# First relational layer: messages made for unsorted edges and carried in the scattered rows

## The reference

```python
def _rel_layer(x, src, dst, etypes, V, a, w_loop, bias, activation=None):
    W = jnp.einsum('rb,bio->rio', a, V)
    seg = dst.astype(jnp.int32) * R + etypes.astype(jnp.int32)
    agg = jax.ops.segment_sum(x[src], seg, num_segments=N * R)
    agg = agg.reshape(N, R, -1)
    h = jnp.einsum('nri,rio->no', agg, W) + x @ w_loop + bias
...
h = _rel_layer(h, src, dst, etypes, V1, a1, loop1, b1, activation=jax.nn.relu)
h = _rel_layer(h, src, dst, etypes, V2, a2, loop2, b2, activation=None)
```

## Time and profile before

| | us |
|---|---|
| median of the timed runs | 3510.24 |
| lowest and highest of them (3 runs) | 3508.18, 3512.7 |
| profiled execution: span from the first to the last instruction | 4186.2 |

### The profile page before, as it was taken

How to read it: one execution, slowest core, us unless ns; L and a number is a source line. 1 busy time by engine, 2 the same in 40 slices (tenths; PEclk the granted TensorE clock), 3 DMA queues, 4 the chain that set the end, 5 groups by cost and what they waited for, 6 DMA issues and landing times. The chain is left out here.

```text
span 4186.2 us, 55154 instructions
## 1 busy us (share of the span) xinstructions
PE 2723.7 (65%) x18509; PEld 1820.0 (43%) x18619; DVE 2656.6 (63%) x8007; ACT 533.4 (13%) x1242; POOL 2327.0 (56%) x2253
## 2 busy tenths in 40 slices
PE   0221001898895888957886899999994555555551
PEld 0100001676663676735554566666652222222221
DVE  9001002888854888868887688888854666665667
ACT  0000000000010000000100222222211222222220
POOL 3777774666606666446664566666725444444430
PEclk9555555777765777778887899999985667676665
DMA  5111002111111111111111000000000000000010
GB/s 88 39 37 26 7 7 62 21 21 21 19 62 38 21 22 22 13 22 23 24 24 16 10 10 10 11 10 11 11 4 21 16 17 17 17 17 16 18 14 4
DMA packets 125021, 91.49 MB, mean 22 GB/s; under 512 B 59542, under 2 KB 110678, under 8 KB 124118
## 3 DMA queue, kind: packets, MB, share of 16 engines
q0 software_dynamic: 70912, 41.10, 7.4%
q1 hardware_dynamic: 53846, 46.89, 4.7%
HBM read 60.42 MB, written 27.41 MB: 21 GB/s over the span
## 5 line engine op out<-in xcount | busy, mean ns | idle before, releaser
L732 POOL DMA_INDIRECT rel_rows<-message_table,message_indices x640 | 647.7, 1012 | 449.7 <-issue 173.8
L1287 POOL DMA_INDIRECT flow_x<-node_table,src_indices x440 | 524.9, 1193 | 293.4 <-PE p_x_turned L1406 153.7
L1655 POOL DMA_INDIRECT att_kv_rows<-kv_table,att_index x440 | 417.5, 949 | 474.4 <-DVE att_index L1666 342.7
L795 DVE TENSOR_SCALAR rel_source_onehot<-rel_sources,node_numbers 128x384 bf16<-128x384 f16 x2000 | 547.4, 321 | 208.3 <-remote 174.1
L393 POOL DMA_INDIRECT sorted_edges<-stage,sorted_row x416 | 429.6, 1033 | 191.7 <-issue 126.3
L1429 PE MATMUL flow_acc_bwd<-flow_onehot_j,flow_by_q 128*128 128x309 bf16 (+1 forms) x2530 | 516.9, 335 | 7.1 <-issue 0.2
L870 PE MATMUL p_rel_picked<-rel_source_onehot,rel_h_parts 128*96 128x384 bf16 x2000 | 458.4, 400 | 33.7 <-issue 24.6
L1691 DVE TENSOR_REDUCE att_tile_max<-p_att_scores 128x4 f32<-128x512 f32 x440 | 292.2, 688 | 236.6 <-PE p_att_scores L1805 166.9
L1038 POOL DMA_INDIRECT sum_rows<-node_table,src_indices x280 | 277.5, 991 | 220.5 <-issue 75.0
L870 PEld LDWEIGHTS p_rel_picked<-rel_source_onehot,rel_h_parts 128*96 128x96 bf16 x2000 | 309.2, 155 | 176.6 <-issue 33.3
L1073 DVE TENSOR_SCALAR sum_source_onehot<-sum_sources,node_numbers 128x512 bf16<-128x512 f16 x1000 | 309.1, 377 | 24.8 <-remote 24.8
(11 more groups left out here) (287 smaller groups left out, 4502.7 us busy)
## 6 DMA issues: line engine op xcount, KB each, us to landing
message_table<-message_rows SPq DMA_DIRECT2D x50, 320.0 KB, 2.1
rel_rows<-message_table,message_indices POOLq DMA_INDIRECT x640
rel_sources<-source_rows SPq DMA_DIRECT2D x80, 96.0 KB
flow_x<-node_table,src_indices POOLq DMA_INDIRECT x440
att_kv_rows<-kv_table,att_index POOLq DMA_INDIRECT x440
sorted_edges<-stage,sorted_row POOLq DMA_INDIRECT x416
sum_sources<-source_rows SPq DMA_DIRECT2D x40, 128.0 KB
sum_rows<-node_table,src_indices POOLq DMA_INDIRECT x280
```

The lines of the kernel that those rows point to most:

```text
L732: pool.indirect_dma_start(out=rows[b][:, t, :], out_offset=None, in_=d["messages"], in_offset=bass.IndirectOffsetOnAxis(ap=s["idx_msg"][:, ...
L795: last = dve.tensor_scalar(which[g % 2][:, c, :], srcs[b][:], s["node"][:, c:c + 1], None, ALU.is_equal)
L1287: pool.indirect_dma_start(out=X[b][:, t, 0:F], out_offset=None, in_=d["nodes"], in_offset=bass.IndirectOffsetOnAxis(ap=s["idx_src"][:, g * ...
L1655: pool.indirect_dma_start(out=KV[b][:, t, :], out_offset=None, in_=d["kv"], in_offset=bass.IndirectOffsetOnAxis(ap=ibuf[b][:, t:t + 1], ax ...
```

## The change

The message of an edge doesn't depend on the order of the edges, so the change makes layer 1's messages ahead of the sort's scatter, for the columns of unsorted edges. A group is now 6 of the 416 columns: the messages of 4 are picked by multiplication (one-hots and picks of 512 edges instead of 384), those of 2 are gathered from the table, and the 6 rows of 52 words (20 as before, then the 32 of the message) are scattered. There are 69 groups and a tail of 2 gathered columns, and 6 ring slots of 6 columns each between making and scattering. The table of layer 1 must now be complete before the first gather, so it is made beside the sort: the matrices of both layers on POOL, the copies and the transfers on ACT. `add_sorted` replaces the pass of layer 1: SP loads the sorted rows with messages (20 contiguous loads), DVE makes the one-hots of the destinations, PE adds. Edge rows, indices and block limits for the later layers stand at its end. The rows that no edge fills are written ahead by one SP transfer that repeats a small tile of zeros. `add_up_pass` stays as it was for layer 2, without the branches for layer 1.

```diff
...
-SB = 4
+ROW = REC + F
+CG, CP, SLOTS, RINGS = 6, 4, 6, 4
+CN = EC // CG
+CTAIL = EC - CN * CG
+CW = CP * P
+PADS = 5
+assert CP + CTAIL <= CG and T % PADS == 0
...
+                                 a["L0_gnn_V1"].rearrange("b i o -> i b o")).then_inc(basis_in, 16)
+                sp.dma_start(ab[:], a["L0_gnn_a1"]).then_inc(basis_in, 16)
+                sp.wait_ge(recs, 2)
+                sp.dma_start(d["sorted"][0:T * P, :].rearrange("(p g t) w -> p g (t w)", p=P, t=PADS),
+                             pad[:].rearrange("p t w -> p (t w)").unsqueeze(1)
+                             .to_broadcast([P, T // PADS, PADS * ROW])).then_inc(pads, 16)
...
+                make_weights(pool)
+                second[2](pool)
+
+                for b in range(2):
+                    pool.wait_ge(out[b], 16 * len(range(b, NB, 2)))
+                pool.wait_ge(index_ready, 1)
...
+                def gather(g):
+                    b = g % SLOTS
+                    slot_free(pool, g)
+                    js, c0 = columns(g)
+                    for j in js:
+                        if j >= CP:
+                            c = c0 + j - js[0]
+                            pool.indirect_dma_start(
+                                out=ring[b][:, j, REC:ROW], out_offset=None, in_=d["messages"],
+                                in_offset=bass.IndirectOffsetOnAxis(ap=idx[:, c:c + 1], axis=0))\
+                                .then_inc(gathered[b], 16)
+
+                def scatter(g):
+                    b = g % SLOTS
+                    js, c0 = columns(g)
+                    pool.wait_ge(filled, g + 1)
+                    if g < CN:
+                        pool.wait_ge(msg_ready, g + 1)
+                    pool.wait_ge(gathered[b], 16 * (CG - CP) * (g // SLOTS + 1))
+                    for j in js:
+                        c = c0 + j - js[0]
                         pool.indirect_dma_start(
                             out=d["sorted"], out_offset=bass.IndirectOffsetOnAxis(ap=row[:, c:c + 1], axis=0),
-                            in_=stage[:, c, :], in_offset=None).then_inc(sent[c % SB], 16)
...
+                            in_=ring[b][:, j, :], in_offset=None).then_inc(sent[b], 16)
+
+                gather(0)
+                pool.wait_ge(row_ready, 1)
+                pool.wait_ge(pads, 16)
+                for g in range(CN + 1):
+                    if g < CN:
+                        gather(g + 1)
+                    scatter(g)
+                for b in range(SLOTS):
+                    pool.wait_ge(sent[b], 16 * sum(len(columns(g)[0]) for g in range(b, CN + 1, SLOTS)))
...
+                for b in range(NB):
+                    if b >= 2:
+                        act.wait_ge(out[b % 2], 16 * (b // 2))
+                    for j in range(2):
+                        act.wait_ge(made, 2 * b + j + 1)
+                        act.copy(y[b % 2][:, j * half:(j + 1) * half], py[(2 * b + j) % 3][:, 0:half]).then_inc(got, 1)
+                    act.wait_ge(got, 2 * b + 2)
+                    act.dma_start(d["messages"].rearrange("(n r) f -> n (r f)", r=R)[b * P:(b + 1) * P, :],
+                                  y[b % 2][:]).then_inc(out[b % 2], 16)
...
+                for g in range(CN):
+                    act.wait_ge(pick_done, g + 1)
+                    if g >= 2:
+                        act.wait_ge(z_done, g - 1)
+                    act.copy(gT[g % 2][:], pp[g % 2][0:3 * F, 0:CW]).then_inc(pick_taken, 1)
+                    act.wait_ge(coef_done, g + 1)
+                    if g >= 2:
+                        act.wait_ge(z_taken, g - 1)
+                    act.copy(coef[g % 2][:].rearrange("p t b -> p (t b)"), pc[:, 0:CP * NBASIS]).then_inc(coef_taken, 1)
+                    fill(g)
+                fill(CN)
...
+                dve.wait_ge(ln_std, 1)
+                v.done(dve.reciprocal(stat[:, 3, :], stat[:, 2, :]))
+                dve.scalar_tensor_tensor(out=h3, in0=c3, scalar=0.0, in1=bc(3), op0=ALU.max, op1=ALU.mult)\
+                    .then_inc(h_ready, 1)
+                for b in range(NB):
+                    last = dve.scalar_tensor_tensor(out=rank[:, b, :], in0=rank[:, b, :],
+                                                    scalar=off[:, b:b + 1], in1=mask[:, b, :],
+                                                    op0=ALU.add, op1=ALU.mult)
+                v.done(last)
...
+                dve.tensor_tensor(row[:, FULL:EC], row[:, FULL:EC], extra[:], ALU.add).then_inc(row_ready, 1)
...
+                def sources(g):
+                    b = g % RINGS
+                    dve.wait_ge(row_in[b], 32 * (g // RINGS) + 32)
+                    if g >= 2:
+                        dve.wait_ge(pick_done, g - 1)
+                    for c in range(NB):
+                        last = dve.tensor_scalar(which[g % 2][:, c, :], srcs[b][:], s["node"][:, c:c + 1], None,
+                                                 ALU.is_equal)
+                    last.then_inc(which_ready, 1)
...
+                def types(g):
+                    if g >= 2:
+                        dve.wait_ge(coef_done, g - 1)
+                    dve.tensor_scalar(kinds[g % 2][:], typs[g % RINGS][:], s["lane"][0:R, 0:1], None, ALU.is_equal)\
+                        .then_inc(kinds_ready, 1)
...
+                def weigh(g):
+                    dve.wait_ge(z_done, g + 1)
+                    dve.wait_ge(coef_taken, g + 1)
+                    if g >= 1:
+                        dve.wait_ge(msg_ready, g)
+                    dve.tensor_tensor(terms[:], pz[:, 0:CP * NBASIS * F]
+                                      .rearrange("p (t f b) -> p t f b", b=NBASIS, f=F),
+                                      coef[g % 2][:].unsqueeze(2).to_broadcast([P, CP, F, NBASIS]), ALU.mult)\
+                        .then_inc(z_taken, 1)
+
+                def messages(g):
+                    dve.wait_ge(z_taken, g + 1)
+                    slot_free(dve, g)
+                    dve.tensor_reduce(ring[g % SLOTS][:, 0:CP, REC:ROW], terms[:], AX_X, ALU.add).then_inc(msg_ready, 1)
+
+                for g in range(CN):
+                    sources(g)
+                    if g >= 2:
+                        weigh(g - 2)
+                    types(g)
+                    if g >= 2:
+                        messages(g - 2)
+                for g in range(CN - 2, CN):
+                    weigh(g)
+                    messages(g)
+
...
+                pe.wait_ge(taken, TURNS)
+                pe.wait_ge(w_ready, 1)
+                w2 = W[:].rearrange("p r f -> p (r f)")
+                for n in range(2 * NB):
+                    b, j = divmod(n, 2)
+                    if n >= 3:
+                        pe.wait_ge(got, n - 2)
+                    pe.matmul(py[n % 3][:, 0:half], s["hT"][0:F, b * P:(b + 1) * P], w2[:, j * half:(j + 1) * half],
+                              start=True, stop=True).then_inc(made, 1)
...
+                def pick(g):
+                    pe.wait_ge(which_ready, g + 1)
+                    if g >= 2:
+                        pe.wait_ge(pick_taken, g - 1)
+                    for c in range(NB):
+                        last = pe.matmul(pp[g % 2][0:3 * F, 0:CW], hs[:, c].rearrange("p k f -> p (k f)"),
+                                         which[g % 2][:, c, :], start=(c == 0), stop=(c == NB - 1))
+                    last.then_inc(pick_done, 1)
+
...
+                for g in range(CN):
+                    pick(g)
+                    if g >= 1:
+                        basis_products(g - 1)
+                    coefficients(g)
+                basis_products(CN - 1)
...
+def add_sorted(nc, a, s, d, sb, ps, sem, init, finish):
...
+                    for c in range(LOADS):
+                        b = c % LBUFS
+                        if c >= LBUFS:
+                            sp.wait_ge(used, (c - LBUFS + 1) * per)
+                            sp.wait_ge(rec_taken, c - LBUFS + 1)
+                            sp.wait_ge(dst_taken, c - LBUFS + 1)
+                        sp.dma_start(rows[b][:].rearrange("p t w -> p (t w)"),
+                                     lanes_rows[:, c * LT:(c + 1) * LT, :].rearrange("p t w -> p (t w)"))\
+                            .then_inc(rows_in[b], 16)
...
+                    for c in range(LOADS):
+                        b = c % LBUFS
+                        dve.wait_ge(rows_in[b], 16 * (c // LBUFS) + 16)
+                        dve.tensor_copy(s["dstl"][:, c * LT:(c + 1) * LT], rows[b][:, :, DSTL]).then_inc(dst_taken, 1)
+                        dve.wait_ge(dst_taken, c + 1)
+                        for g in range(c * per, (c + 1) * per):
+                            if g >= HBUFS:
+                                dve.wait_ge(used, g - HBUFS + 1)
+                            dve.tensor_tensor(hot[g % HBUFS][:], lanes[:].unsqueeze(1).to_broadcast([P, RG, P]),
+                                              s["dstl"][:, g * RG:(g + 1) * RG].unsqueeze(2)
```

(64 more changed lines are left out.)

576 lines of the change are left out of this document (333 added, 243 removed).

## The result

The changed kernel takes 3535.98 us (median of 4 runs, 3532.39 to 3541.3) against 3509.21 before: ratio 1.0079, 95% interval 1.0065 to 1.0093. It is 27 us slower, where 55 less had been forecast. The prediction was wrong in the sign of the change.

What follows compares the result with a forecast made beforehand. POOL alone bounded the scatters, mostly DVE and PE pass 1. New terms 120 + 728 + 10 + 40 + 110 = 1008 against 1060; forecast 55 less, 3455 us (1.6%), range 3400 to 3580.

Steps and rivals of the forecast that it cites:

- The part before: Old kernel up to the end of layer 1's pass: 1205 us profiled, taken as 1060 in timed runs.
- The rival of cheaper indirect DMAs: Old scatters: the 0.30 between indirect DMAs is added by profiling; old part 935 against 1008, total 3583; chance 0.06.
- The first gather: Start of the new kernel until layer 1's table is whole: 52 for normalised nodes plus 67 for the table, taken as 120.
- the bound of 150: Upper bound for the first gather, if POOL's 30 matrix instructions hold DVE up for 30 us.
- The groups and the last scatters: New loop: 70 periods of 10.4 us, set by DVE, 728; then one more period, 10, for the last scatters.
- the mean of the earlier trace: One-hots in the new loop at a mean 378 ns each: upper bound of 12.2 a group, 854 in all.
- third rival: New loop: POOL is slowed by DVE's one-hots, 13.5 a group, 946 in place of 728, total 3676; chance 0.05.
- the row of 3.04: Earlier profile row: 10 one-hots of 128x512 took 3.04 with gathers running; gave 7.6 for a group's 25.
- Read-back, limits and the rest: Between and around loop and adds: drain, first load, edge rows, indices and block limits, 40 us, bounds 30 to 60.
- The adds: New stage of 440 adds, two matmuls each, at 0.234 an add: 103, taken as 110 us.
- The fourth rival: Adds take as long as the old pass's last ones: 198 in place of 110, total 3546; chance 0.09.
- point of decision, 162: Length of the adds, 0.37 each, from which the rival of slow adds decides.

Runs made afterwards that it cites:

- the first profile: Profile of the unchanged kernel before, in a slower execution: span 4186.2 us, against a median of 3510.24 in the timed runs.
- the second profile: The kernel before, with no edit, profiled once more in an execution as fast as the timed ones: time 3507.72 us, span 3505.9.

## Why the prediction was wrong, by its own steps

**The part before.** Taken as 1060; measured 1060. Taking out of the first profile what no engine's work explained was right: the second one has 530 for the scatters and 413 for pass 1, where the prediction's deductions leave 526 and 417, and POOL has no wait above 0.3 in the middle of that pass. The rival of cheaper indirect DMAs is out: scatters stand at 0.96 and 0.30 in the second profile too (416 in 530), and that execution lasted as long as the timed ones.

**The first gather: 120, measured 139.** The mechanism that was named for the bound of 150 came: POOL's matrices held up DVE's sort, by 26.5 in the masks (37.00 against 10.46), and the scan held up POOL. What failed is the reason given for leaving this out, that the fill ends before the long steps. The fills run until 8.16, beside the first masks (from 4.47), and cost them some 3 by the comparison above (10.46 against 7.23); the matrices ran from 8.24 to 76.2, beside the rest of the masks and past the scan. The nodes came at 78 in place of 52, and the first gather followed after 61 instead of 67. Moving the matrices gave 24 back in all.

The Trainium skill, page "SBUF — State Buffer", section "Who interferes with whom", has VectorE and GpSimd lock each other out of a shared port pair for a whole instruction, if VectorE's is in a two-port mode, or has two inputs in SBUF while GpSimd's reads SBUF. The trace agrees where both compute: the POOL instruction of 22.93 ends 1.3 after the scan that started 1.2 ahead of it, and 25 masks took 37.00 beside the matrices and 10.46 without them (in which mode the masks ran no row shows). For indirect DMAs the section speaks of GpSimd starved; here it was DVE that paid, 7.65 against 6.63 in a group, with POOL's step unchanged at 1.27.

**The groups and the last scatters: 728 and 10, measured 728 together.** The start-to-start time of the one-hots beside gathers was the right row (0.304 in the sum, 0.306 measured), the mean of the earlier trace rows the wrong one. POOL's starving (third rival) didn't come. That the engines were level is right for DVE and POOL: 10.23 and eight steps of 1.27. The sum took DVE as the longest; in the changed kernel neither waits for the other in the middle of the loop, and POOL ends last. What indirect DMAs cost DVE was already in the row of 3.04, which was taken beside one.

**Read-back, limits and the rest: 40, measured 36.** There are 21.7 from the last scatter's end to the first add and 14 behind the last.

**The adds: 110, measured 188.** This is the step that failed and that turned the sign. Two rows for the same instructions differed by a factor of two, and the sum took the faster one because 440 adds in a row leave PE no pause. That reason is what the runs refute: a PE without a pause did not have the higher clock. In the pass of before, adds stood among picks at a mean clock of 0.83 (1.00 around the row that was used); alone, they run at 0.50 though PE never waits. The fourth rival had the place, the price (198) and the row (the last adds of the pass, behind the last picks), and its point of decision, 162, was passed. Its chance of 0.09 was too low: the row nearest to the new stage, adds with no other work beside them, was the slow one. With the adds at 103 to 110 the kernel would by the sum be some 50 faster than before, as forecast. That the rest of the sum would then fit is partly luck: 19 too little for the first gather, 10 too much for the loop and 4 too much for the read-back nearly cancel.

## What to carry to other kernels

When a change moves matmuls out of a mix into a stage of their own, price them by the row in which they already ran alone, and look up the granted clock of that stretch: here the same adds cost 0.43 alone and 0.23 in the mix. A stage of small f32 matmuls can be cheaper as one bf16 matmul over three parts, even at the lower clock. And instructions moved to POOL aren't free beside DVE: here 30 small ones cost the sort's masks 26 us.

## What the runs showed that had not been expected

Useless work saved time: 320 more matmuls of 512 columns took the adds from 188 to 144, with the granted clock at 0.99 in place of 0.50. The same remedy in the tables cost 85, with the clock at 0.55. And indirect DMAs, which cost POOL 1.27 each, also cost DVE time when it makes one-hots beside them: 1.0 in a group with eight of them.
